# Causal attention stages: the penalty above the diagonal moves from TensorE to VectorE and GpSimd

## The reference, cut to what matters

```python
energy = jnp.einsum('bhsk,bhtk->bhst', Q, K)
energy = jnp.where(cols[None, None, None, :] >= lengths[:, :, None, None], -jnp.inf, energy)
if causal:
    energy = jnp.where(cols[None, :] > cols[:, None], -jnp.inf, energy)
score = jax.nn.softmax(energy / jnp.sqrt(dk), axis=-1)
out = jnp.einsum('bhst,bhtk->bhsk', score, V)
```

## Time and profile before

| what | value |
| --- | --- |
| median of three runs | 3414.09 us |
| the profiled execution | 3420.81 us |
| its span | 3419.0 us |
| PE busy | 3026.8 us (89%) |
| DVE busy | 1914.5 us (56%) |
| ACT busy | 1492.1 us (44%) |
| POOL busy | 451.8 us (13%) |

### The profile page before, as it was taken

How to read it: one execution, slowest core, us unless ns; L and a number is a source line. 1 busy time by engine, 2 the same in 40 slices (tenths; PEclk the granted TensorE clock), 3 DMA queues, 4 the chain that set the end, 5 groups by cost and what they waited for, 6 DMA issues and landing times. The chain is left out here.

```text
span 3419.0 us, 47618 instructions
## 1 busy us (share of the span) xinstructions
PE 3026.8 (89%) x17126; PEld 1808.1 (53%) x17248; DVE 1914.5 (56%) x4677; ACT 1492.1 (44%) x2134; POOL 451.8 (13%) x538
## 2 busy tenths in 40 slices
PE   6888888856999999989999999996999999978686
PEld 3444333342444444379898989993444444347353
DVE  4666777654767776443333333334777777734354
ACT  1333444521555555544444444431555555543233
POOL 0111111143211111010000000001122221113112
PEclk7889888976999999989999999997999999998798
DMA  4212121103222222000000000003222222100331
GB/s 116 49 40 57 46 64 46 30 1 70 76 61 82 67 77 60 18 25 26 26 25 26 26 26 26 1 1 69 78 61 87 58 76 58 30 1 1 83 86 49
DMA packets 75113, 162.66 MB, mean 48 GB/s; under 512 B 15401, under 2 KB 21673, under 8 KB 72697
## 3 DMA queue, kind: packets, MB, share of 16 engines
q1 hardware_dynamic: 74872, 159.51, 17.8%
HBM read 60.76 MB, written 2.10 MB: 18 GB/s over the span
## 5 line engine op out<-in xcount | busy, mean ns | idle before, releaser
L883 ACT ACTIVATE probT_a<-scores 128x1024 f32<-128x1024 f32 (+3 forms) x832 | 785.1, 949 | 841.8 <-PE scores L737 469.8
L992 DVE CUSTOM_DVE_ANT_0 ring<-ring,maskb_a 128x512 f32<-128x512 f32 x1024 | 681.9, 719 | 204.8 <-PE ring L754 175.1
L754 PE MATMUL ring<-stacks_a 64*128 64x512 f32 (+7 forms) x1664 | 451.9, 422 | 72.2 <-DMA stacks_a<-fixed_a 26.0
L1329 DVE TENSOR_TENSOR hidden_moe<-whole_moe,hidden_moe 128x512 fp32r<-128x512 f32 x288 | 199.8, 694 | 519.9 <-ACT whole_moe L1251 519.7
L775 PE MATMUL outputs<-probT_a,V_a 128*32 128x512 f32 (+6 forms) x3328 | 451.1, 586 | 23.9 <-ACT probT_a L883 11.8
L1172 PE MATMUL scores<-tokens_moe,weights_moe 128*128 128x512 f32 x1728 | 447.8, 395 | 4.9 <-issue 4.9
L719 PE MATMUL scores<-stacks_a 64*128 64x512 f32 (+7 forms) x1664 | 415.6, 480 | 0.0
L719 PEld LDWEIGHTS scores<-stacks_a 64*128 64x128 f32 (+1 forms) x1664 | 166.4, 188 | 464.0 <-issue 344.9
L990 DVE TENSOR_REDUCE negm_a<-ring 128x1 f32<-128x512 f32 (+3 forms) x640 | 329.7, 562 | 144.5 <-PE ring L760 103.2
L1185 PE MATMUL ring<-weights_moe,hidden_moe 128*128 128x256 f32 x2592 | 402.8, 283 | 4.0 <-DVE hidden_moe L1329 3.4
L1185 PEld LDWEIGHTS ring<-weights_moe,hidden_moe 128*128 128x128 f32 x2592 | 367.6, 191 | 30.7 <-issue 4.6
(11 more groups left out here) (151 smaller groups left out, 3240.7 us busy)
## 6 DMA issues: line engine op xcount, KB each, us to landing
stacks_a<-parts_a SPq DMA_DIRECT2D x672, 128.0 KB
raw<-in_moew SPq DMA_DIRECT2D x9, 2048.0 KB, 7.5
maski_a<-in_mask SPq DMA_DIRECT2D x16, 1024.0 KB, 5.3
wt<-in_w SPq DMA_DIRECT2D x7, 1024.0 KB, 5.0
kvT_a<-in_ctxT SPq DMA_DIRECT2D x12, 512.0 KB, 3.5
stacks_a<-fixed_a SPq DMA_DIRECT2D x4, 1024.0 KB
wrow<-in_row SPq DMA_DIRECT2D x7, 512.0 KB, 6.2
stacks_a<-mrow_a SPq DMA_DIRECT2D x224, 8.0 KB
```

The source lines that it names most:

```text
L754: last = pe.matmul(bank("S", j, n, e)[:, 0:w], Q[rows, g, qt * P:(qt + 1) * P], K[rows, g, 0:w], start=True, stop=not a.causal)
L883: act.activation(probT[:, kb % 2, 2 * p:2 * p + 2, q0:S], scores_bank(j, n)[:, :, q0:S], ACT.Exp, bias=0.0, scale=-1.0).then_inc(c_exp.sem, 1)
L992: least = dve.tensor_tensor_reduce(sc, sc, maskb[:, m % 2, qt, :], 1.0, BIG * 2, ALU.add, ALU.min, out)
L1329: dve.tensor_tensor(hidden[:, m % 4, 1, :], whole[:, m % 2, :], hidden[:, m % 4, 0, :].bitcast(F32), ALU.subtract).then_inc(c_low.sem, 1)
```

## The change

In causal stages the four bf16 matmuls of a half go. VectorE now takes the minimum with the instruction that the masked stages use (a custom instruction and a read of its accumulator), adding a tile `cmask` as it goes: zeros for all but the last 128 columns, and the penalty tile `causal` there. The exponential is taken of scores without a penalty; GpSimd then writes zeros over what lies above the diagonal in the block of 128 queries by two heads (`affine_select`), and `PV` waits for that (`c_tri`) in place of the exponential. `cmask` is built on VectorE before its first work, behind a wait for all six constant transfers. The work `ln` is cut in two on GpSimd: L690 and L692 stay, and gain and shift become the work `gain`, one half later.

```diff
@@ timetable
-                (qt + (5 if a.wo else 3), "ln", -1, qt)]
+                (qt + (5 if a.wo else 3), "ln", -1, qt), (qt + (6 if a.wo else 4), "gain", -1, qt)]
@@ gpsimd
+                if kind == "exp":
+                    m, _ = divmod(j, 4)
+                    _, _, a, _ = stage_of(m)
+                    if a.causal:
+                        kb, p = divmod(n, couples)
+                        q0 = a.since(kb)
+                        own = probT[:, kb % 2, 2 * p:2 * p + 2, q0:q0 + P]
+                        pool.wait_ge(*c_exp.at(j, n))
+                        pool.affine_select(own, own, [[0, 2], [1, P]], ALU.is_ge, 0.0, 0, -1).then_inc(c_tri.sem, 1)
...
+                if kind == "gain":
+                    _, b, _, k = stage_of(j)
+                    r = n % 2
                     pool.wait_ge(*c_centred.at(j, n))
                     pool.tensor_tensor(xh[:, r, :], xh[:, r, :], wrow[:, k, 2, :], ALU.mult)
@@ tensor, key_penalties
-                    if a.causal:
-                        last = pe.matmul(out[:, q0:q0 + P], causal[:, :], identb[:, :], start=False, stop=True)
@@ tensor, query_scores
-                if a.causal:
-                    for e in range(2):
-                        pe.matmul(bank("S", j, n, e)[:, w - P:w], identb[:, :], causal[:, :],
-                                  start=False, stop=True).then_inc(c_ring.sem, 1)
+                    pe.matmul(bank("S", j, n, e)[:, 0:w], Q[rows, g, qt * P:(qt + 1) * P],
+                              K[rows, g, 0:w], start=True, stop=True).then_inc(c_ring.sem, 1)
@@ tensor, outputs
-                pe.wait_ge(*c_exp.at(j, (kb + 1) * couples - 1))
+                done = c_tri if a.causal else c_exp
+                pe.wait_ge(*done.at(j, (kb + 1) * couples - 1))
@@ vector
             dve.memset(mx[:, :, :, :].bitcast(F32), 0.0)
+            if a0.causal:
+                dve.memset(cmask[:, 0:S - P], 0.0)
+                dve.wait_ge(c_const, 96)
+                dve.tensor_copy(cmask[:, S - P:S], causal[:, :])
...
-                        if a.mask is None:
+                        if a.mask is None and not a.causal:
                             least = dve.tensor_reduce(out, sc, AX.X, ALU.min)
                         else:
-                            least = dve.tensor_tensor_reduce(sc, sc, maskb[:, m % 2, qt, :], 1.0, BIG * 2, ALU.add,
-                                                             ALU.min, out)
+                            more = cmask[:, S - w:S] if a.causal else maskb[:, m % 2, qt, :]
+                            least = dve.tensor_tensor_reduce(sc, sc, more, 1.0, BIG * 2, ALU.add, ALU.min, out)
```

More of the change, by code:

```diff
@@ L159, in wanted @@
     n = int(st[1:])
-    return {"ot": a.wo, "y": a.wo, "ln": a.ln, "len": a.length, "maskld": a.mask is not None,
+    return {"ot": a.wo, "y": a.wo, "ln": a.ln, "gain": a.ln, "len": a.length, "maskld": a.mask is not None,
             "maskcv": a.mask is not None, "mT": a.mask is not None, "cnld": a.kv == "mctx",
@@ L438, in attention_block @@
             maskT = sb("maskT", [P, 2, QT, S], BF16)
+        if a0.causal:
+            cmask = sb("cmask", [P, S], BF16)
         if length:
@@ L475, in attention_block @@
                 c_exp.mark(j, n)
+                if att[units[j // 4][0]].causal:
+                    c_tri.mark(j, n)
             if kind == "PV":
@@ L620, in _ @@
                     load_expert(sp, ORDER[ORDER.index(stages[-1]) + 1], 0)
-                if kind == "ln" and last and n == QT - 1:
+                if kind == "gain" and last and n == QT - 1:
                     _, b, _, _ = stage_of(j)
@@ L719, in key_scores @@
                     last = pe.matmul(scores_bank(j, h)[:, e, q0:S], K[rows, g, kb * P:(kb + 1) * P],
-                                     Q[rows, g, q0:S], start=True, stop=not (a.causal or a.mask is not None))
-                if not (a.causal or a.mask is not None):
+                                     Q[rows, g, q0:S], start=True, stop=a.mask is None)
+                if a.mask is None:
                     last.then_inc(c_st.sem, 1)
@@ L728, in key_penalties @@
                 kb, _ = divmod(h, couples)
-                q0 = a.since(kb)
-                if a.mask is not None and u == 0 and h == 0:
+                if a.mask is None:
+                    return
+                if u == 0 and h == 0:
                     pe.wait_ge(*c_rA.at("mT", m, QT - 1))
                 for e in range(2):
-                    out = scores_bank(j, h)[:, e, :]
-                    if a.causal:
-                        last = pe.matmul(out[:, q0:q0 + P], causal[:, :], identb[:, :], start=False, stop=True)
-                    if a.mask is not None:
-                        last = pe.matmul(out, identb[:, :], maskT[:, m % 2, kb, :], start=False, stop=True)
-                if a.causal or a.mask is not None:
-                    last.then_inc(c_st.sem, 1)
+                    last = pe.matmul(scores_bank(j, h)[:, e, :], identb[:, :], maskT[:, m % 2, kb, :],
+                                     start=False, stop=True)
+                last.then_inc(c_st.sem, 1)
             def query_scores(j, n):
@@ L753, in query_scores @@
                     bank_free("S", j, n, e)
-                    last = pe.matmul(bank("S", j, n, e)[:, 0:w], Q[rows, g, qt * P:(qt + 1) * P],
-                                     K[rows, g, 0:w], start=True, stop=not a.causal)
-                    if not a.causal:
-                        last.then_inc(c_ring.sem, 1)
-                if a.causal:
-                    for e in range(2):
-                        pe.matmul(bank("S", j, n, e)[:, w - P:w], identb[:, :], causal[:, :],
-                                  start=False, stop=True).then_inc(c_ring.sem, 1)
+                    pe.matmul(bank("S", j, n, e)[:, 0:w], Q[rows, g, qt * P:(qt + 1) * P],
+                              K[rows, g, 0:w], start=True, stop=True).then_inc(c_ring.sem, 1)
             def outputs(j, kb):
```

9 lines of the change are left out of this document (5 added, 4 removed).

## The result

Twelve runs of the changed kernel took 3421.3 us in the median (3414.5 to 3428.1), beside 3412.2 us for the kernel before on the same chip (3406.7 to 3419.2). The ratio is 1.0025, with an interval of 1.0014 to 1.0036: slower by 9 us. Forecast were 3390 us, and 3364 to 3420 us as the range. The sign was wrong, and the time lies outside the range.

The account below looks back on a forecast made before the run. TensorE was taken as nearest to the bound, not alone in setting the pace, with VectorE the bound at batch boundaries. 45 - 8 - 4 - 7 - 2 = 24 us less gave 3390 us, 80% range 3364 to 3420 us.

Parts of the forecast that it names:

- 45 of 54 us on the path: Causal stages a0 and a6: 192 penalty groups at 0.28 us make 54 us; 9 us in batch boundaries excluded, 45 gained.
- 21 us of costs: Sum of forecast losses: PV waits 8 us in a0 and 4 in a6, batch boundaries 7, head 2.
- What of it lies in a batch boundary is worth nothing: In a0 and a6 boundaries TensorE waits for VectorE, so 33 halves, 9 us of removed matmuls, gain nothing.
- B: Rival: VectorE paces both stages, the 45 us shrink to some 20, 3414 us; chance 0.18 together with C.
- C: Rival: new gaps on TensorE lower a0's clock, costing 25 us, 3415 us; chance 0.18 together with B.
- The rule on the clock: TensorE's clock is throttled by default and activity releases it, so removing TensorE work could take back the gain.
- rival A: GpSimd's zeros take 1.5 us each, delaying PV and boundaries by 36 us: slower, 3426 us; chance 0.12.
- The `PV` waits: PV waiting for GpSimd's zeros in units without cover: 13 x 0.6 us in a0, 13 x 0.3 in a6.
- I take 1.2 us a boundary, six of them: 7 us: At a0 and a6 batch boundaries, zeros ahead of gain and variance in GpSimd's queue delay VectorE's centring.
- 0.04 to 0.06 us a piece: VectorE's custom minimum takes that much longer for each of 384 pieces, most of it beside TensorE's work.
- The head: At kernel start VectorE waits for six constants and builds cmask; first projection at 12.85 us instead of 10.84, 2 us lost.
- The signs: Right if a0 is some 14 us shorter, a6 some 10; wrong if a0's clock is under 0.8 or a1 to a5 change.

Follow-up runs that it names:

- e2: The kernel before with all causal penalty matmuls left out and nothing in their place, so unmasked, for timing only; 3400.8 us, ratio 0.9941.
- e6: The changed kernel without the writes of zeros, PV waiting for the exponential again, for timing only; 3404.3 us, ratio 0.9965.
- e10: e2 with four bf16 filler matmuls in one group ahead of each half's ST, which overwrites them; 3411.0 us, ratio 0.9989.
- e5: The changed kernel with GpSimd's context scaling later and a bf16 filler matmul ahead of each score product, which overwrites it; 3520.9 us, ratio 1.0303.
- e12: The changed kernel with GpSimd's context scaling later and variance and power ahead of the zeros of their half; 3407.2 us, ratio 0.9972.
- e7: e3 with the building of cmask moved behind the first copy of xT; 3409.8 us, ratio 0.9984 to the kernel before.
- e3: The changed kernel with only the VectorE part: custom minimum with cmask, ST's penalties kept on TensorE, no zeros; 3408.9 us, ratio 0.9976 to the kernel before.

## Why the prediction was wrong

**The sum, term by term.** Forecast were 45 of 54 us on the path, and 21 us of costs. Measured by ratios: 20 us of gain (e2), and costs of 8 (custom minimum with the head) and 20 (zeros and their queue), +8.5 us before rounding. These are the steps from before to after by way of e2 and e6, so they must add up to the result; that they do is no proof.

**The step that failed is the first one**: "What of it lies in a batch boundary is worth nothing ... That leaves 45 us." It took all work outside the boundaries for time on the path, and the clock for fixed. At the full clock a unit of a0 won 1.2 of 2.2 us, and a6 won 10.7 of 18: 18 + 11 = 29 us. In the halves with wide minima TensorE waits for VectorE, as the timeline of after shows; that this is the whole of the missing half was not tested. Of these 29 the clock of a0 took some 12, by the estimate above. The rest, 17, with 2 us of head, makes about the 20 that e2 gained. Both parts stood in the prediction as rivals, B and C, as if only one of them could hold and with 0.18 for both; both held, in half of their size. Two smaller things in the same term were off as well. In the rows at the full clock a group took 0.42 us out of the stream and not 0.28, so more work was removed than the 54 us and still less came back. And work in a boundary was not worth nothing: the three units with a boundary became 1.8, 1.2 and 0.1 us shorter in e2.

**The rule on the clock.** In a0, less of TensorE's work went with a lower clock (0.88 to 0.80, e2) and work put back went with a higher one (0.80 to 0.88, e10). The Trainium skill, page "TensorE: Matmul & The Clock Gate", section "Part 1: The HAM clock gate", says that the clock is throttled by default and that activity releases it; these two agree. e5, busy for 94% of a0 at 0.76, doesn't, if activity is read as the busy time of the profile.

**The zeros.** The duration was too high (0.75 for 0.41 us), which made the costs look safe; rival A, a slow write, did not come. The `PV` waits were priced at 12 us and cost about 3 (e12 against e6). "I take 1.2 us a boundary, six of them: 7 us" named the right mechanism: e12 shows 9 us in the two stretches, 1.5 us a boundary, of which the waits confirm those of a6. What the prediction did not have is the scaling of the context with its wait for a transfer, 10 us by the ratios and 4 in the trace. It asked what stood in front of the variance, and not what stood in front of the zeros. The Trainium skill, page "Perfetto Trace Analysis", section "Tensor Engine Instruction (MATMUL, LD_WEIGHTS)", calls GpSimd "strict FIFO", and the rows of 277.00 and 278.85 us show it.

**The minimum.** By its own 0.04 to 0.06 us a piece it had 15 to 23 us of VectorE's time, and put them in the sum at nothing, "most of it beside TensorE's work". In a0 that cost 7 us by the traces, where the wide minima are the pace in the rows above; in a6, where a minimum is needed half as often, nothing.

**The head.** 2 us forecast, 2.4 measured (e7), though the first projection came 1.85 us later than forecast.

**The signs.** `S` to `ST` under 0.3 us and longer centring waits came as named, and only told that the instructions behaved. The zeros took 0.41 us, under the 0.6 to 0.9 named, and the first projection started at 14.70 us, not near 12.9. The two signs that bear on the time failed: a0 is 10 us longer, not 14 shorter, and a6 3.7 us shorter, not 10. Of those for "wrong", the clock of a0 under 0.8 came true, 0.73 in the same stretch. The waits of `PV` for GpSimd come near the 20 us named: 15 us for its weight loads in the two stages, and another 6 for its products, which in part lie at the same time. Whether a1 changed, as a further sign would have it, stays open.

## What to carry to other kernels

Before work on TensorE is counted as gain, look at the granted clock of the stretch and at who waits there: at 0.98 (a6) six tenths of the removed time came back, at 0.88 (a0) a sixth. These are two stages of one kernel, not a law. An instruction that others wait for, put into an engine's queue, inherits every wait ahead of it, also those for transfers that hindered nobody before; and what stood behind it in the queue is later too. Here one moved line and one reordered pair were worth 18 us by the ratios, twice what the change had lost.

## What the runs showed of the hardware

- The clock doesn't go by the busy time alone. In a0 it stood at 0.88 with TensorE busy for 85% (before, e10), at 0.80 for 80% (e2), at 0.77 for 79% (after), but at 0.76 for 94% (e5). e5 differs from the others by single products of 64 rows with a bf16 matmul between each; whether that is why its clock stayed low was not tested. What the chip counts is open.
- Two matmuls on different rows ran as one where they stood next to each other, 0.34 us for a pair of `S` with 384 columns, and one after the other, about 0.6 us each, with a matmul over all rows between (e5).
- VectorE's instruction on 4 elements took 2.65 us and the copy behind it 2.57, instead of 0.17 and 0.69 us, when they came while GpSimd's fill of `V` was under way (10.99 us, 3.51 long). Both end at 14.53, just behind it at 14.50. e3 has the same, and in e7, where they ran ahead of the fill, they took 0.17 and 0.69 us again. The reduction over 1024 elements at 10.59 us was hardly touched (1.21 us, 1.16 before). The Trainium skill, page "SBUF — State Buffer", section "Who interferes with whom", says that copies and operations with a scalar can take a port pair which VectorE shares with GpSimd as an exclusive lock, and that reductions never do. The trace agrees for the instruction on 4 elements, which takes a scalar, and for the reduction. The copy reads a bank of PSUM and came behind that instruction, so whether it was held by itself is not shown. These are the 1.9 us that the head's forecast lacked.
- A write of zeros by a condition on the index costs 0.41 us for 256 elements a partition on GpSimd, less than its product of two tiles of that size (0.73).
